# Attention and quantized FFN on one core: the down product in quarters between the up chunks, and the scores in two column tiles turned back by two transposes

## What is computed

```python
# x: (8, 512, 512), ctx: (8, 64, 512), w1, w2: (2048, 512), w3: (512, 2048)
scores = einsum('bsd,bmd->bsm', layernorm(x), ctx) / sqrt(512)
attn   = softmax(where(mask, scores, -1e30))
x      = x + where(any(mask), einsum('bsm,bmd->bsd', attn, ctx), 0)

def linear_bit(x, w, g):          # quantized linear layer
    xn = g * x * rsqrt(mean(x*x) + 1e-8)
    xq = round(xn * 127 / max|xn|) * max|xn| / 127
    s  = mean(|w|);  wq = round(tanh(w / s)) * arctanh(s)
    return xq @ wq.T
xl = layernorm(x)
h  = silu(linear_bit(xl, w1, g1)) * linear_bit(xl, w2, g2)
x  = x + linear_bit(h, w3, g3)
```

## Time and profile before

| | |
|---|---|
| runs | 470.70, 471.52, 474.17 us, median 471.52 |
| profiled execution | 472.33 us, of which the span of the instructions is 470.5 |
| mean granted clock of PE | 0.942 of full speed |
| busy, share of the span | PE 87%, DVE 87%, POOL 73%, ACT 72% |

### The profile page before, as it was taken

One profiled execution on the slowest core, in us unless ns is written; L12 is line 12 of the kernel. 1 busy time (PEld: TensorE's weight loads), 2 busy tenths in 40 slices (PEclk: granted clock), 3 DMA queues, 4 the chain that ended last, 5 costly groups with the idle time before them and its releaser, 6 DMA issues. The chain is left out here.

```text
span 470.5 us, 8445 instructions
## 1 busy us (share of the span) xinstructions
PE 409.9 (87%) x1966; PEld 197.5 (42%) x1966; DVE 407.1 (87%) x927; ACT 339.5 (72%) x607; POOL 341.3 (73%) x539
## 2 busy tenths in 40 slices
PE   8326644899999999999999999999999999999995
PEld 8102412344644464446434543445444634334432
DVE  3799576889899999999999999999999999999662
ACT  1585446986798769886988788878886796666552
POOL 0267858787777787788788787778777877878650
PEclk9756795899999999999999999999999999999998
DMA  7999901545557455745574466447654444444431
GB/s 270 396 366 421 312 16 22 135 90 114 139 148 173 90 114 143 179 88 115 165 178 89 111 182 163 90 111 189 139 129 111 91 88 91 86 94 91 90 69 45
DMA packets 110504, 67.45 MB, mean 143 GB/s; under 512 B 100752, under 2 KB 100880, under 8 KB 106768
## 3 DMA queue, kind: packets, MB, share of 16 engines
q1 hardware_dynamic: 110480, 67.19, 53.9%
HBM read 34.14 MB, written 8.39 MB: 90 GB/s over the span
## 5 line engine op out<-in xcount | busy, mean ns | idle before, releaser
L521 POOL TENSOR_TENSOR stageB<-stageB,g3b 128x512 f32<-128x512 f32 x128 | 163.8, 1285 | 46.2 <-DVE stageB L907 45.3
L1163 PE MATMUL S<-W2q,q12T 128*128 128x512 f16 x512 | 134.5, 386 | 8.9 <-DVE stageB L907 6.2
L1163 PE MATMUL S<-W1q,q12T 128*128 128x512 f16 x512 | 135.3, 388 | 0.0
L693 ACT ACTIVATE sg<-S,asc 128x512 f32<-128x512 f32 x128 | 87.5, 683 | 54.1 <-PE S L1163 49.3
L1191 PE MATMUL DN<-W3q,stageB 128*128 128x512 f16 x512 | 118.7, 386 | 7.3 <-DMA stageB<-stageB 7.3
L907 DVE TENSOR_TENSOR stageB<-sg,S 128x512 f32<-128x512 f32 x128 | 86.7, 677 | 19.9 <-ACT sg L693 10.5
L913 DVE TENSOR_REDUCE hm<-stageB 128x1 f32<-128x512 f32 x128 | 86.5, 677 | 0.2 <-POOL stageB L521 0.2
L1163 PEld LDWEIGHTS S<-W2q,q12T 128*128 128x128 f16 x512 | 49.5, 99 | 75.3 <-DVE stageB L907 13.9
L1191 PEld LDWEIGHTS DN<-W3q,stageB 128*128 128x128 f16 x512 | 49.8, 99 | 70.3 <-issue 10.8
L1163 PEld LDWEIGHTS S<-W1q,q12T 128*128 128x128 f16 x512 | 49.8, 100 | 66.3 <-issue 10.1
L685 ACT ACTIVATE stageB<-stageB,hf 128x1024 f16<-128x1024 f32 x64 | 69.8, 1140 | 4.8 <-DVE hf L933 4.8
(11 more groups left out here) (112 smaller groups left out, 430.7 us busy)
## 6 DMA issues: line engine op xcount, KB each, us to landing
xTs<-in_xT SPq DMA_DIRECT2D x8, 1024.0 KB, 7.0
X<-in_x SPq DMA_DIRECT2D x8, 1024.0 KB, 6.0
out_x<-X SPq DMA_DIRECT2D x32, 256.0 KB, 2.9
X<-in_w1T SPq DMA_DIRECT2D x4, 1024.0 KB, 12.5
stageB<-in_w2T SPq DMA_DIRECT2D x4, 1024.0 KB, 20.4
X<-in_w3T SPq DMA_DIRECT2D x4, 1024.0 KB, 9.2
ctxr<-in_ctx SPq DMA_DIRECT2D x16, 128.0 KB, 3.1
ctxc<-in_ctx SPq DMA_DIRECT2D x8, 128.0 KB, 3.9
```

The source lines that it names most:

```text
L521: nc.gpsimd.tensor_tensor(gh[q][:, part], hp[:, part], g3b[:, part], ALU.mult).then_inc(s_gh_made, 1)
L693: nc.scalar.activation(sg[n % 2][:, :], S1[n % 2][:, :], ACT.Silu, scale=asc[z][:, 0:1])\
L1163: mm = nc.tensor.matmul(bank[n % 2][:, :], q12T[q][:, i * KD + k, :], w[:, n, k, :], start=(k == 0), stop=(k == KD - 1))
```

## The change

Two things move, and a third goes with them.

**Down in quarters.** `down(t, first, count)` now does some of four quarters of four matmuls. In a slot, quarter 0 stands behind up chunk 0, quarter 1 behind chunk 1, quarters 2 and 3 behind chunk 2. A new semaphore `s_down_top` counts the first two quarters; the DMA transpose of the first half of `q3T` waits for it, that of the second half for the whole product. DVE's `result` moves from before gate(2) (before gate(1) in slot 1) to before gate(3), and `worth_3` to one `max_3` ahead of it.

**Scores in two column tiles.** The context is now the stationary operand, 64 columns of it, and 256 tokens move at a time: the tokens of groups 0 and 2 go to the array's columns 0 to 63 and those of groups 1 and 3 to columns 64 to 127. Eight fp32 matmuls instead of 16 write a result that has the context positions on partitions. ACT copies it to a new tile `half` (`attention_half`), and PE turns it back with two fp32 transposes of 128 x 128 (`attention_turn`) into the place in R[1] that the softmax reads. The load of the next `xTs` and the copy of the next `ccT` wait for the scores as they are before the turn.

Not shown are the declarations of `half`, `s_half_ps`, `s_half_made` and `s_down_top`.

```diff
--- before.py
+++ after.py
...
@@ -319,7 +323,7 @@
 
             def load_xT(a):
                 if later(a):
-                    sp.wait_ge(s_scores_ps, a)
+                    sp.wait_ge(s_half_ps, a)
                     sp.nop(nofuse=True)
                 sp.dma_start(xTs[:, :, :, :].rearrange("p k j q -> p (k j q)"), xT[a]).then_inc(s_xT_in, 16)
 
@@ -346,7 +350,7 @@
                 sp.wait_ge(s_c3_made, NHALF * t + h + 1)
                 sp.nop(nofuse=True)
                 if later(t):
-                    sp.wait_ge(s_down_ps, t)
+                    sp.wait_ge(s_down_ps if h else s_down_top, t)
                 sp.nop(nofuse=True)
                 sp.dma_start_transpose(q3T[:, h * HB:(h + 1) * HB, :], c3[:, h * HALF:(h + 1) * HALF])\
                     .then_inc(s_q3_in[h], 16)
@@ -628,8 +632,14 @@
             def attention_ccT(a):
                 act.wait_ge(s_ccT_ps, a + 1)
                 if later(a):
+                    act.wait_ge(s_half_ps, a)
+                nc.scalar.copy(ccT[:, :, :].rearrange("p k m -> p (k m)"), CT[:, :]).then_inc(s_ccT_made, 1)
+
+            def attention_half(a):
+                act.wait_ge(s_half_ps, a + 1)
+                if later(a):
                     act.wait_ge(s_scores_ps, a)
-                nc.scalar.copy(ccT[:, :, :].rearrange("p k m -> p (k m)"), CT[:, :]).then_inc(s_ccT_made, 1)
+                nc.scalar.copy(half[:, :], R[1][:, 0:TPB // 2 * P]).then_inc(s_half_made, 1)
 
             def attention_exp(a):
                 act.wait_ge(s_rs_made, a + 1)
@@ -724,6 +734,7 @@
             act.wait_ge(s_const_ones, 1)
             table(0, ACT.Exp)
             attention_ccT(0)
+            attention_half(0)
             weight_abs(0, stageA, 0, s_w1_abs)
             attention_exp(0)
             attention_probT(0)
@@ -773,6 +784,7 @@
                 if prep and j == 2:
                     two(x_sum, b + 2, 2)
                 if attn and j == 0 and not first:
+                    attention_half(b + 1)
                     two(x_square, b + 1, 2)
                 busy = attn and j in (0, 2) or first and j == 1
                 if not busy:
@@ -784,6 +796,7 @@
                     silu(t, 2, j % NZ)
                 if first and j == 0:
                     weight_abs(2, stageA, 1, s_w3_abs)
+                    attention_half(1)
                 if first and j == 1:
                     for h in range(NHALF):
                         quantize_3(0, h, 0)
@@ -1038,9 +1051,6 @@
                     stage_a_factor(1, 1)
                 if ahead and not (first and j == 0):
                     stage_a_gain(t + 2)
-                if not early and j == 1:
-                    worth_3(t - 2, j % 2)
-                    result(t - 2)
                 gate(t, 1)
                 if first and j == 0:
                     weight_clip(W2f, 3, s_w2_pool, 2, s_w2_q)
@@ -1050,14 +1060,13 @@
                     weight_abs(2, stageA, 2, s_w3_abs)
                     weight_mean(2, WC)
                     weight_scale(2, stageA, W3f, 1, s_w3_dve)
-                if not early and j != 1:
-                    worth_3(t - 2, j % 2)
-                    result(t - 2)
                 if attn and j < 3:
                     stage_a_max(t + 2)
                 if first and j == 1:
                     stage_h_factor(0, 0, 0)
                 gate(t, 2)
+                if not early:
+                    worth_3(t - 2, j % 2)
                 if ahead and not (attn and j < 3):
                     stage_a_max(t + 2)
                 max_3(t, 0, j % 2)
@@ -1065,6 +1074,8 @@
                     attention_norm(1)
                     weight_clip(W3f, 0, s_w3_act, 1, s_w3_q)
                     weight_clip(W3f, 1, s_w3_dve, 1, s_w3_q)
+                if not early:
+                    result(t - 2)
                 gate(t, 3)
                 if attn and j == 0:
                     attention_softmax(b + 1)
@@ -1118,10 +1129,16 @@
                 if later(a):
                     pe.wait_ge(s_x1_made, TPB * a)
                 pe.wait_ge(s_xT_in, 16 * (a + 1))
-                for j in range(TPB):
-                    for k in range(KD):
-                        mm = nc.tensor.matmul(R[1][:, j * M:(j + 1) * M], xTs[:, k, j, :], ccT[:, k, :],
-                                              start=(k == 0), stop=(k == KD - 1))
+                for k in range(KD):
+                    for e in range(2):
+                        mm = nc.tensor.matmul(R[1][e * M:(e + 1) * M, 0:TPB // 2 * P], ccT[:, k, :], xTs[:, k, e::2, :],
+                                              start=(k == 0), stop=(k == KD - 1), tile_position=(0, e * M))
+                mm.then_inc(s_half_ps, 1)
+
+            def attention_turn(a):
+                pe.wait_ge(s_half_made, a + 1)
+                for i in range(TPB // 2):
+                    mm = nc.tensor.transpose(R[1][:, i * P:(i + 1) * P], half[:, i * P:(i + 1) * P], identf[:, :])
                 mm.then_inc(s_scores_ps, 1)
 
             def attention_probT(a):
@@ -1175,27 +1192,32 @@
                         if k in (HB - 1, 3 * HB // 2 - 1, KH - 1):
                             mm.then_inc(s_q3_ps, 1)
 
-            def down(t, turned=False):
-                if later(t):
+            def down(t, first=0, count=WC, turned=False):
+                quarter = KH // WC
+                if first == 0 and later(t):
                     pe.wait_ge(s_x2_made, t)
-                for k in range(KH):
-                    if turned:
-                        if k == 3 * HB // 2:
-                            pe.wait_ge(s_q3_act, 1)
-                        elif k % (HB // 2) == 0:
-                            pe.wait_ge(s_q3_dve, k // (HB // 2) + 1)
-                    elif k % HB == 0:
-                        pe.wait_ge(s_q3_in[k // HB], 16 * (t + 1))
-                    if not later(t) and k % (KH // WC) == 0:
-                        pe.wait_ge(s_w3_q, k // (KH // WC) + 1)
-                    mm = nc.tensor.matmul(DN[:, :], q3T[:, k, :], W3q[:, k, :], start=(k == 0), stop=(k == KH - 1))
-                mm.then_inc(s_down_ps, 1)
+                for g in range(first, first + count):
+                    if turned and g == 3:
+                        pe.wait_ge(s_q3_act, 1)
+                    elif turned:
+                        pe.wait_ge(s_q3_dve, g + 1)
+                    elif g % 2 == 0:
+                        pe.wait_ge(s_q3_in[g // 2], 16 * (t + 1))
+                    if not later(t):
+                        pe.wait_ge(s_w3_q, g + 1)
+                    for k in range(g * quarter, (g + 1) * quarter):
+                        mm = nc.tensor.matmul(DN[:, :], q3T[:, k, :], W3q[:, k, :], start=(k == 0), stop=(k == KH - 1))
+                    if g == 1:
+                        mm.then_inc(s_down_top, 1)
+                    if g == 3:
+                        mm.then_inc(s_down_ps, 1)
 
 
             for i in range(20):
                 nc.tensor.matmul(DN[:, 0:P], ones[:, :], ones[:, :], start=True, stop=True)
             attention_ccT(0)
             attention_scores(0)
+            attention_turn(0)
             attention_probT(0)
             attention_readout(0, 0)
             weight_total(0, s_w1_abs, WC + 1)
@@ -1209,9 +1231,12 @@
                 up(t, 0, q)
                 if attn and j == 0 and not first:
                     attention_ccT(a)
-                if not (first and j < 2):
-                    down(t - 2)
+                turn = not (first and j < 2)
+                if turn:
+                    down(t - 2, 0, 1)
                 up(t, 1, q)
+                if turn:
+                    down(t - 2, 1, 1)
                 if attn and j == 0:
                     if first:
                         attention_ccT(a)
@@ -1224,9 +1249,15 @@
                 if attn and j == 2:
                     attention_readout(a, 1)
                 up(t, 2, q)
+                if turn:
+                    down(t - 2, 2, 2)
                 if first and j == 0:
                     attention_scores(a)
+                if attn and j == 0 and not first:
+                    attention_turn(a)
                 up(t, 3, q)
+                if first and j == 0:
+                    attention_turn(a)
                 if attn and j == 1:
                     attention_readout(a, 0)
                 if first and j == 1:
@@ -1234,7 +1265,7 @@
             batches(pe, slot)
             down(NT - 2)
             turn_3(NT - 1)
-            down(NT - 1, True)
+            down(NT - 1, turned=True)
 
 
 # ---- launch ----
```

4 lines of the change are left out of this document (added).

## The result

The changed kernel takes 456.56 us (median of 4 runs, 455.24 to 456.90), the kernel before 472.00 beside it (4 runs, 470.70 to 474.17). The profiled execution took 456.24 us with a span of 454.4, against 472.33 and 470.5 before, so 16.1 us are to be accounted for.

The account below looks back on a forecast made before the run. DVE was taken to bound the loop, with PE held back. Gains of 5 x 1.0 + 0.9 + 4.3 + 1.7 + 0.4 = 12.3 us from 472.33 gave a forecast of 460 us, 8-in-10 range 454.5 to 467.

Parts of the forecast that it names:

- DVE sets the loop's pace: Loop batches: DVE runs back to back and holds PE back; PE's saving of 1.6 us a batch buys nothing by itself.
- PE will only wait longer for L907, up to 2.5 us: Loop batches: PE's 1.1 us wait for DVE's gate product grows to as much as 2.5 us a batch.
- The holes, 1.0 us a batch: DVE's hole behind hsc, 0.22 to 0.30 us in each of four slots, goes with the new order: 1.0 us a batch.
- The loop, 5.0 us: Five loop batches, each 1.0 us shorter by DVE's closed holes.
- ACT's stall, 0.2 to 0.3 us: Slot 0: gate(2) waits 0.2 to 0.3 us for ACT, late from the scores, in place of 0.22 before.
- Column tiles overlap, loads hidden: Scores: 16 records in two column tiles run together with weight loads covered, 1.95 us instead of 3.52.
- Rival 1: Scores: column tiles don't overlap but loads are hidden, scores take 3.4 us, total 471 us; chance 0.08.
- Rival 2: Scores: weight loads are bare as well, scores take 6.4 us, total 492 us; chance 0.06.
- Rival 3, the loop falls to PE's sum of 46.7: Loop: DVE is not the wall, a batch falls to PE's summed work of 46.7 us, total 450 us; chance 0.08.
- The last batch, 4.3 us: Last batch: PE's four 1.1 us waits for the q3T DMA transpose go, gaining 4.3 us, bounds 3 and 4.6.
- Batch 0, 2.1: Batch 0: 1.7 us from DVE's shorter wait for chunk 3 behind the scores, 0.4 from its later slots.
- Rival 4: Loop gives nothing, ACT's stall or longer DVE operations eat the gain; batch 0 and last batch pay, 466 us; chance 0.15.

Follow-up runs that it names:

- e1: The kernel before with only the new scores, half copy and turn; down product and DVE order as before: 473.70 us, ratio 1.0039.
- e4: The changed kernel with worth_3 (output scale) again directly ahead of result, which stays at its new place: 463.57 us, ratio 0.9820.
- e13: The changed kernel with one 0.216 us product left out of up chunk 1 in each of 32 tiles: 455.81 us, ratio 0.9642.
- e2: The changed kernel with the scores as before (16 matmuls, no copy or turn), quarters and DVE order kept: 462.65 us, ratio 0.9817.
- e3: The kernel before with only DVE's order changed, worth_3 and result at their new places: 469.17 us, ratio 0.9947.
- e7: The changed kernel with ACT's two squares ahead of its copy of half the scores in slot 0: 456.24 us, ratio 0.9679.
- e5: The changed kernel with one column tile's eight score records ahead of the other's, instead of alternating: 462.02 us, ratio 0.9813.
- e10: e7's kernel with DVE's softmax subtraction moved behind the second hidden maximum: 456.10 us, ratio 0.9689.
- e11: The changed kernel with only DVE's softmax subtraction moved behind the second hidden maximum: 455.97 us, ratio 0.9695.
- e8: The changed kernel with worth_3 and result back at their old places, quarters and new scores kept: 469.41 us, ratio 0.9957.

## Why the prediction was right, and where its steps were off

**DVE sets the loop's pace: held.** Saving PE alone gave nothing (e1), DVE's holes put back cost their whole length (e4), taking from PE gave nothing (e13). But "PE will only wait longer for L907, up to 2.5 us" was wrong: it waits for L907 never. With the down product in quarters PE's work is spread evenly, and its slack gathers at the one place where it needs the exponentials, 1.1 us. And "nothing by itself" was right of the scores only by themselves; behind the quarters they are worth 0.45 us a batch (e2). Once DVE's holes are closed, PE with the old scores is the next wall: DVE waits for it 1.3 us a batch in e3 and 0.9 in e2. The prediction counted the closed holes in full and did not ask whether PE would deliver without its saving.

**The holes, 1.0 us a batch: 1.2.** The two bounds of 0.22 and 0.30 were there, and the right one was the upper, since 0.42 less 0.12 is what passes from `hsc` to the next start.

**The loop, 5.0 us: 6.9.** This is the term that was most mis-sized. A batch like that of the earlier trace rows became 1.26 us shorter, and the sum by lines of the views gives it: holes 1.2, `ga` 7.2 to 6.9, the subtraction 0.80 to 0.73, less 0.4 for ACT's stall (0.22 to 0.60). I counted operations as if they kept their length. The five give 5 x 1.26 = 6.3. The other 0.6 is in the first of the five alone: before it took 50.09 us (112.78 to 162.87), 0.64 more than each of the rest and not "within half a microsecond" of them, with a wait of DVE for PE of 1.0 in it, and afterwards it takes 48.18 like the others.

**ACT's stall, 0.2 to 0.3 us: 0.6.** The chain was right: worked out, the scores ended 5.9 us and the gate could start 10.5 us behind the batch's CT transposes (218.2 and 222.8 less 212.31), and the trace has 6.0 and 10.6 (213.10 and 217.66 less 207.07). Off was DVE, which stands ready 10.0 us behind them and not 10.2, and waits that much longer. The prediction's own list had half a microsecond at this gate as a sign of being wrong, and the sign came true. It cost nothing, though, as e7 shows: POOL's product covered it, which the prediction did not know, so here the time came out right by luck. That the cover is thin was right: every 0.1 us of scores more costs DVE 0.1 us, by e5 over 0.9 us.

**Column tiles overlap, loads hidden: held.** 1.88 us for the scores, forecast 1.95. Rival 1 would have come true if the records had not alternated, but at 2.8 us and not 3.4. Rival 2 fell. The source line's view of the loop batch:

```profile
L1134 PEld LDWEIGHTS R<-xTs,ccT x16: 132/137/138, 211.1 to 212.5; 128*64 128x64 f32 x16
L1134 PE MATMUL R<-xTs,ccT x16: 378/379/429, 211.1 to 212.7; 128*64 128x256 f32 x16
```

Sixteen weight loads of 0.137 us would be 2.2 us by themselves, more than the group takes. The rule of the Trainium skill that loads overlap only matmuls in another row group ("TensorE: Matmul & The Clock Gate", What overlaps and what doesn't) does not hold for these two tiles, which share theirs; the same page also says, further up (Step-by-step: what each phase is for), that a load may be pulled ahead into the array's background buffer, and that is what the trace agrees with.

**Rival 3, the loop falls to PE's sum of 46.7:** it did not; the batch is 48.2. PE's busy time came out at 47.09.

**The last batch, 4.3 us: 4.4; batch 6, 0.9: 1.0.** The start was right at 0 as well: DVE's softmax there starts within 0.1 us of before's (13.38, before 13.49), behind its own statistics.

**Batch 0, 2.1: 2.1, but not by the terms.** The gate that answers to the earlier trace rows, then the stretch in which the scores stand ahead of it:

```profile
59.20 0.69 DVE L920 TENSOR_TENSOR stageB<-sg,S 128x512 f32<-128x512 f32 x1 [2.97 <-PE S L1180]
...
54.00:58.00 4.00, 4.00 (x22) 1.73 (x21) 1.28 (x2) 2.45 (x4) 2.83 (x12) 0.76 1.01 420
```

The wait is shorter by 1.0 us, not by 1.55: at a granted clock of 0.76 the scores take 2.43 us here (54.76 to 57.19) and not 1.95. The other 1.1 come in the later slots, for which I had counted 0.4. That the sum is right is luck, and it is the sum of one execution: e7, e10 and e11 have the same order in batch 0 and come to the CT transposes of batch 1 at 111.39, 109.62 and 109.38 us, against 110.69.

**The end, 0: 1.6.** A step that was missing. Rows of the profiled execution of before showed the last product at 4.84 us where the one ahead took 3.6; this execution had a low clock at its end, and I took its length for a fixed one. How much of this is in the medians is not known: a profile shows one execution.

**Rival 4** (the loop gives nothing) is what e8 shows for quarters and scores without the new order: there the loop batch is even 0.9 us longer than before, and only batch 0 and the last batch pay.

## What to carry to other kernels

Work out who holds a loop by what its waits say, not by who is busiest, and then ask for each thing that you free who is next: here PE's saving was worth nothing until DVE's order was better, DVE's order was worth a third of itself until PE's work was spread, and together they gave all of it. A busy time is not yet work: where an elementwise operation takes 0.42, 0.73, 1.01 and 1.39 us with the same shape, look at what runs beside it on the other engine, since its records hide a wait that no view of waits shows. And when a stall is found, look at whether another path of the same length runs beside it before you count its removal as a gain.
